# Expert choice behind the score transposes, rank products behind the value products, v ahead of q, and POOL's sum between its scatters

## What is computed

```
x  = x + fp8_ffn(lora_linear(x, cond_8))               # layer 0, gives x1
z  = x1 @ w_bot(cond_8) + bias                         # layer 1, one mixed weight per sequence
hn = layernorm(z);  q, k, v = hn @ wq, hn @ wk, hn @ wv
attn = softmax(q k / sqrt(8)) over 32 keys, 16 heads;  x' = z + attn v @ wo + bo
hn2 = layernorm(x');  idx = argmax(hn2 @ gate_w + gate_b)   # 8 experts, one per token
y  = x' + w2[idx] @ relu(w1[idx] @ hn2 + b1[idx]) + b2[idx];  out = x1 + y
```

## Time and profile before

| | |
|---|---|
| median of 3 runs | 324.71 us (321.15 to 331.06) |
| the profiled execution | 325.63 us, of it 323.8 us from the first to the last instruction |
| busy share of the span | PE 80%, DVE 67%, POOL 62%, ACT 60% |
| passes 5, 6 (L754 to the next L754) | 22.13 us, 21.47 us |
| granted TensorE clock, mean | 0.913 |

### The profile page before, as it was taken

The page is one execution under the profiler, slowest core; times in us unless marked ns, Lnnn a source line. Parts: engine busy times, 40 slices in busy tenths (PEclk is TensorE's granted clock), DMA queues, the critical chain, the costliest instruction groups (busy, mean ns, idle before and its releaser), DMA issues.

```text
span 323.8 us, 10450 instructions
## 1 busy us (share of the span) xinstructions
PE 259.3 (80%) x3558; PEld 201.6 (62%) x3565; DVE 215.6 (67%) x596; ACT 195.4 (60%) x422; POOL 199.4 (62%) x270
## 2 busy tenths in 40 slices
PE   4797889979979879799685876885849299999970
PEld 1454555755845656567465556774839289999970
DVE  4731499897988988988969777764743215565630
ACT  1556788795986986968946627325424036666640
POOL 1323265587786887887687655656674316878770
PEclk9977999999999999999988598579987859999996
DMA  5359100102002002010010051030241332333200
GB/s 191 121 170 436 47 3 2 37 0 79 25 10 90 0 33 81 0 65 5 2 65 5 2 157 43 2 95 29 80 142 50 101 88 55 99 93 104 89 22 0
DMA packets 12042, 22.01 MB, mean 68 GB/s; under 512 B 2508, under 2 KB 8656, under 8 KB 11744
## 3 DMA queue, kind: packets, MB, share of 16 engines
q1 hardware_dynamic: 8640, 14.63, 14.2%
q0 software_dynamic: 2784, 6.32, 5.7%
q10 hardware_dynamic: 576, 0.53, 0.5%
HBM read 13.97 MB, written 7.95 MB: 68 GB/s over the span
## 4 chain that ended last, share of the span: by engine, by line
PE 49%; DVE 23%; issue 11%; ACT 6%; DMA 4%; POOL 2%; SPq 1%; DVEq 1%; ACTq 0%; POOLq 0%
PE d L401 7%; PE d L413 6%; PE so L729 6%; PE so L401 5%; DVE mx L1171 5%; DVE pt L1189 4%; PE so L413 4%; DMA pack_sb<-pack 2%; PE d L805 2%; PE d L754 2%; PE d L788 2%; DVE pr L1175 2%; PE d L783 2%; PE so L716 2%; PE d L700 2%
## 5 line engine op out<-in xcount | busy, mean ns | idle before, releaser
L633 POOL DMA_INDIRECT out<-ob,rin x39 | 39.8, 1019 | 22.7 <-DVE w1s L551 12.6
L1456 POOL DMA_INDIRECT routed<-rows,slot x32 | 33.1, 1035 | 14.2 <-issue 9.1
L1378 POOL TENSOR_TENSOR t<-pr 128x512 f32<-128x512 f32 x16 | 20.5, 1282 | 15.4 <-ACT pr L958 15.3
L700 PE MATMUL d<-ybd,pack_sb 128*128 128x256 f32 x112 | 29.8, 396 | 0.0
L551 DVE COPY w1s<-pack_sb 128x644 f32 x39 | 22.3, 577 | 9.7 <-issue 4.0
L401 PE MATMUL d<-xt,w1s 128*128 128x128 f32 x168 | 26.8, 308 | 1.7 <-ACT xt L436 0.6
L413 PE MATMUL d<-pack_sb,mid 128*128 x168 | 27.3, 314 | 1.0 <-ACT mid L443 0.8
L436 ACT ACTIVATE xt<-d,pack_sb 128x128 f32<-128x128 f32 x21 | 9.6, 459 | 28.2 <-PE d L385 28.2
L401 PE MATMUL so<-xt,w1s 128*128 128x128 f32 x144 | 21.5, 295 | 6.3 <-issue 5.3
L413 PEld LDWEIGHTS d<-pack_sb,mid 128*128 128x128 f32 x168 | 24.6, 225 | 2.0 <-issue 1.8
L401 PEld LDWEIGHTS d<-xt,w1s 128*128 128x128 f32 x168 | 24.3, 220 | 2.5 <-issue 2.2
(11 more groups left out here) (184 smaller groups left out, 648.9 us busy)
## 6 DMA issues: line engine op xcount, KB each, us to landing
rin<-routed SPq DMA_DIRECT2D x39, 128.5 KB
pack_sb<-pack SPq DMA_DIRECT2D x1, 2576.0 KB, 15.2
xb<-x_t SPq DMA_DIRECT2D x8, 256.0 KB, 3.2
pack_sb<-pack SPq DMA_DIRECT2D x1, 2048.0 KB, 8.5
routed<-pad SPq DMA_DIRECT2D x5, 128.5 KB
out<-ob,rin POOLq DMA_INDIRECT x39
pack_sb<-pack SPq DMA_DIRECT2D x1, 584.0 KB, 6.2
routed<-pad ACTq DMA_DIRECT2D x4, 128.5 KB
```

Source lines behind the costliest of these rows:

```text
L633: pool.indirect_dma_start(out, bass.IndirectOffsetOnAxis(rin[s % 8][:, 2 * H:ROW].bitcast(U32), 0), ob[u][:, :], None, bounds_check=N_TOK ...
L700: mm = pe.matmul(mix_bank(a, k)[:, u * 256:(u + 1) * 256], col[f"mix_w{k // 2}"][:, (blk % 4) * P:(blk % 4 + 1) * P], ybd[:, :, :].rearran ...
L1378: pool.tensor_tensor(t16[:, f, :], e32[:, :, 0:16], e32[:, :, 16:32], ALU.add).then_inc(sem["sums"], 1)
L1456: pool.indirect_dma_start(routed, bass.IndirectOffsetOnAxis(slot[:, g:g + 1], 0), rows[:, g, :], None).then_inc(sem["scattered"], 16)
```

## The change

No operation is added or taken out. Four things move in the written order of the queues:

- DVE: `pick` moves from between the third and the fourth score block to behind the fourth transposition (in all passes that have attention work). `rank` moves from between the third and the fourth transposition to behind `eighth`, and `place` to behind the sum and reciprocal (L1320, L1325), with the first tables and copies of pass 8 behind it.
- TensorE: the rank products move from ahead of the k products to behind the value products. v's products go ahead of `coded`, and q's behind it: the last thing of a pass.
- ACT: the copies of v and q (`v_out`, `q_out`) swap places likewise. q's copy (L1077) was the first after L1073; now the order is reciprocals, v, q, `coded`.
- POOL: `x1` goes between the second and the third scatter, and with it the next pass's `spread`, so that the third and fourth scatter come behind both.

```diff
@@ TensorE @@
-                if m is not None:
-                    wait(pe, "pick", 6 * (m + 1))
-                    ... (rank products) ...
-                    mm.then_inc(sem["rank_mm"], 1)
                 if late(m) and m == NC - 2:
                     turn(2)
                     output(1)
                     hidden(2)
...
                     values(range(0, NG)).then_inc(sem["pv_mm"], 1)
+                if m is not None:
+                    wait(pe, "pick", 6 * (m + 1))
+                    ... (rank products) ...
+                    mm.then_inc(sem["rank_mm"], 1)
-                if n is not None:
-                    if m is not None:
-                        wait(pe, "slot", 5 * m + 2)
-                    pe.matmul(dn[0][:, :], col["wq"], hn_t[:, :], start=True, stop=True).then_inc(sem["qkv_mm"], 1)
-                if a is not None and not (isinstance(a, int) and a == 0):
-                    coded(a, n)
                 if n is not None:
                     wait(pe, "x1_tok", n + 1)
                     ... (v products) ...
                     mm.then_inc(sem["qkv_mm"], 1)
+                if a is not None and not (isinstance(a, int) and a == 0):
+                    coded(a, n)
+                if n is not None:
+                    if m is not None:
+                        wait(pe, "slot", 5 * m + 2)
+                    pe.matmul(dn[0][:, :], col["wq"], hn_t[:, :], start=True, stop=True).then_inc(sem["qkv_mm"], 1)
@@ ACT @@
-                if n is not None:
-                    wait(act, "qkv_mm", 3 * n + 2)
-                    act.activation(qt[:, :], dn[0][:, :], ACT.Identity, bias=col["bq"]).then_inc(sem["q_out"], 1)
                 ... (reciprocals, rcx) ...
+                if n is not None:
+                    wait(act, "qkv_mm", 3 * n + 2)
+                    wait(act, "pv_mm", n)
+                    act.activation(v[:, :, :], groups(dn[3][:, :]), ACT.Copy).then_inc(sem["v_out"], 1)
+                    wait(act, "qkv_mm", 3 * n + 3)
+                    act.activation(qt[:, :], dn[0][:, :], ACT.Identity, bias=col["bq"]).then_inc(sem["q_out"], 1)
                 if a is not None and not (isinstance(a, int) and a == 0):
                     coded(a)
@@ DVE @@
                     shifted(j, 2)
-                if m is not None:
+                if m is not None and j is None:
                     pick(m)
...
-                if m is not None:
-                    rank(m, p)
                 if isinstance(m, int) and m == SNAP:
                     first_pair()
                 if j is not None:
                     turned(j, 3)
+                if m is not None and j is not None:
+                    pick(m)
...
-                if m is not None:
-                    place(m)
-                if isinstance(m, int) and m == SNAP:
-                    first_b()
-                    for s in range(3):
-                        copy(s)
                 if a is not None:
                     eighth(a)
...
+                if m is not None:
+                    rank(m, p)
                 ... (sum, reciprocal) ...
+                if m is not None:
+                    place(m)
+                if isinstance(m, int) and m == SNAP:
+                    first_b()
+                    for s in range(3):
+                        copy(s)
@@ POOL @@
-                    for g in range(NG):
-                        pool.indirect_dma_start(...)
+                    scatter(0)
+                    scatter(1)
                 if a is not None:
                     ... (x1) ...
+                if a is not None and not (isinstance(a, int) and a == NC - 1):
+                    spread(a + 1)
+                if m is not None:
+                    scatter(2)
+                    scatter(3)
```

More of the change, by code:

```diff
@@ L877, in iteration @@
                     mm.then_inc(sem["hn_tr"], 1)
-                if m is not None:
-                    wait(pe, "pick", 6 * (m + 1))
-                    pe.matmul(gates(m)[:, 64:64 + NG * E], upper_b[:, :], oh_b[:, :, :].rearrange("p g e -> p (g e)"),
-                              start=True, stop=False, skip_group_check=True)
-                    for g in range(NG):
-                        mm = pe.matmul(gates(m)[:, 64 + (g + 1) * E:64 + (NG + 1) * E].rearrange("p (g e) -> p g e", e=E),
-                                       ones_b[:, :], oh_b[:, g, :].unsqueeze(1).to_broadcast([P, NG - g, E]),
-                                       start=False, stop=(g == NG - 1), skip_group_check=True)
-                    mm.then_inc(sem["rank_mm"], 1)
                 if late(m) and m == NC - 2:
@@ L914, in iteration @@
                     values(range(0, NG)).then_inc(sem["pv_mm"], 1)
+                if m is not None:
+                    wait(pe, "pick", 6 * (m + 1))
+                    pe.matmul(gates(m)[:, 64:64 + NG * E], upper_b[:, :], oh_b[:, :, :].rearrange("p g e -> p (g e)"),
+                              start=True, stop=False, skip_group_check=True)
+                    for g in range(NG):
+                        mm = pe.matmul(gates(m)[:, 64 + (g + 1) * E:64 + (NG + 1) * E].rearrange("p (g e) -> p g e", e=E),
+                                       ones_b[:, :], oh_b[:, g, :].unsqueeze(1).to_broadcast([P, NG - g, E]),
+                                       start=False, stop=(g == NG - 1), skip_group_check=True)
+                    mm.then_inc(sem["rank_mm"], 1)
                 if late(m) and m == NC - 2:
@@ L1084, in iteration @@
                     normed(3)
+                if n is not None:
[4 more added lines that the diff above has]
+                    act.activation(qt[:, :], dn[0][:, :], ACT.Identity, bias=col["bq"]).then_inc(sem["q_out"], 1)
                 if a is not None and not (isinstance(a, int) and a == 0):
                     coded(a)
-                if n is not None:
-                    wait(act, "qkv_mm", 3 * n + 3)
-                    wait(act, "pv_mm", n)
-                    act.activation(v[:, :, :], groups(dn[3][:, :]), ACT.Copy).then_inc(sem["v_out"], 1)
             def between(act):
@@ L1371, in rstd, with spread, scatter @@
                 pool.tensor_tensor(dst[:, 1, :], dst[:, 0, :], minus_half[:, :], ALU.pow).then_inc(sem[signal], 1)
+            def spread(a):
+                wait(pool, "wb_mm", 4 * a)
+                hold(pool, "held_pool")
+                pool.tensor_tensor(ybd[:, :, :],
+                                   col["y_rep"][:, bass.ds(a * CB, CB)].unsqueeze(1).to_broadcast([P, 16, CB]),
+                                   col["mask_o"].unsqueeze(2).to_broadcast([P, 16, CB]),
+                                   ALU.mult).then_inc(sem["ybd"], 1)
+            def scatter(g):
+                pool.indirect_dma_start(routed, bass.IndirectOffsetOnAxis(slot[:, g:g + 1], 0),
+                                        rows[:, g, :], None).then_inc(sem["scattered"], 16)
             def summed(j, half):
@@ L1388, in iteration @@
                     pool.wait_ge(sem["in1"], 16)
-                if a is not None:
-                    wait(pool, "wb_mm", 4 * a)
-                    hold(pool, "held_pool")
-                    pool.tensor_tensor(ybd[:, :, :],
-                                       col["y_rep"][:, bass.ds(a * CB, CB)].unsqueeze(1).to_broadcast([P, 16, CB]),
-                                       col["mask_o"].unsqueeze(2).to_broadcast([P, 16, CB]),
-                                       ALU.mult).then_inc(sem["ybd"], 1)
+                if isinstance(a, int) and a == 0:
+                    spread(0)
                 if isinstance(m, int) and m == SNAP:
@@ L1454, in iteration @@
                     hold(pool, "held_pool")
-                    for g in range(NG):
-                        pool.indirect_dma_start(routed, bass.IndirectOffsetOnAxis(slot[:, g:g + 1], 0),
-                                                rows[:, g, :], None).then_inc(sem["scattered"], 16)
+                    scatter(0)
+                    scatter(1)
                 if a is not None:
```

## The result

Changed kernel: median 339.84 us (6 runs, 335.77 to 344.86); kernel before, same chip: 328.13 us (6 runs). Ratio 1.049, 95% interval 1.033 to 1.065: slower. The profiled execution took 340.3 us against 325.63, 14.7 us more.

A forecast was written before the change was run, and what follows sets the result against it. No single engine bounds the loop; a ring of steps crossing engines does. Terms 2.5 + 3.4 + 1.8 + 3.5 + 1.5 = 12.7 us, against the median 324.71, gave 337.4, stated as 337.5 us; range 329.5 to 343.5.

The forecast's parts named there:

- the ring: Chain of steps crossing the engines, followed through pass 5, claimed to set the length of a loop pass.
- `rstd` "fits, with 0.3 to spare": POOL, loop passes: scatters end at V + 11.5, `rstd` due at V + 11.8; no cost, bound 0.5 us per pass.
- V sooner by 0.44: Loop passes: V, the start of the value products, comes 0.44 us sooner, limited by ACT's last exponential.
- q last, loop: Passes 3 to 6: q's late copy puts L754 at V + 5.8, `o_t` at V + 7.5; +3.4 us net.
- Passes 1 and 2: Front, without `pick`: v and `coded` stand ahead of q, nothing comes sooner; +2.5 us, bounds 1.0 and 3.0.
- Pass 7, "level": Pass 7's end: taken as unchanged, since with no further `a` no L754 follows its q.
- Pass 8, POOL: Pass 8: two scatters are put ahead of the tables of counts before `rstd`; +1.8 us, bounds 1.2 and 2.4.
- Pass 8, DVE: Pass 8: `rank` waits for rank products behind the values, postponed work delays the heads; +3.5 us, bounds 2.3 and 3.8.
- Pass 9: DVE: `place`, sum and reciprocal move behind the rank products, after the values' end; +1.5 us, bounds 0.5 and 1.8.
- ACT waits for the scatter to land: Passes 4 to 8: late scatter signal delays ACT's normalization row and exponentials 1 us each; +5, 342.5 us; chance 0.12.
- early values carry through: Passes 3 to 9: earlier value products take 1.4 us off each, q's copy hidden; 314.9 us; chance 0.03.
- only the front pays: Passes 8 and 9: TensorE hides POOL's table count and DVE's late work; only 5.9 us lost, 330.6; chance 0.14.

The follow-up runs named there:

- first pair: First profiles of the changed kernel and the kernel before, both unmodified: 340.3 us against 325.63.
- last chip: Both kernels run again unmodified: changed kernel 331.50 us, ratio 1.051; kernel before profiled again, 313.67 us (one run).
- v/q run: Kernel before with only the v/q order change on TensorE and ACT: 332.71 us, ratio 1.013.
- v/q runs: v/q order change alone on the kernel before, 332.71 us, ratio 1.013; and undone in the changed kernel, 335.81 us, ratio 1.049.
- late-passes run: Changed kernel with choice, rank products, `rank`, `place`, tables and copies of passes 8 to 10 put back: 332.36 us, ratio 1.035.

## Why the prediction was right or wrong

The direction and the ring were right, and the sum, 12.7 us, lies near the 14.7 of the two profiles. The step that failed is the one that put nothing down for the way behind `o_t`: `rstd` "fits, with 0.3 to spare". `o_t` to `nmr2` grew by 0.9 to 1.2 us in passes 4 to 6, which is 3.0 of the loop's 5.0 us, and by 0.9 in pass 7; the steps that had a price in the loop gave 2.0 us for 3.4. That the sum came near is in part luck, as errors in both directions met in it:

| us more than before | said | first pair | last chip |
|---|---|---|---|
| up to the first `o_t` | 2.5 | 2.3 | 2.4 |
| passes 3 to 6 | 3.4 | 5.0 | 5.3 |
| pass 7 | 0 | -0.2 | 1.3 |
| pass 8 | 5.3 | 6.2 | 5.2 |
| pass 9 | 1.5 | 3.2 | 0.8 |
| the rest | 0 | -1.8 | 1.8 |
| sum | 12.7 | 14.7 | 16.7 |

On the last chip the kernel before had one loop pass that was 1.6 us longer than its others; without it the loop's 5.3 would be 6.9.

- **V sooner by 0.44**: measured 0.5 to 0.6, with DVE idle ahead of the last transposition.
- **q last, loop**: L754 at V + 5.64 (said 5.8), reciprocals at V + 3.8 (3.7), `o_t` at V + 7.27 (7.5). Right, and shown alone by the v/q run. The reading "now 6.37" held 0.9 us of a late copy that other chips don't have; there the same step costs 1.8. One reading was wrong: in the kernel before `o_t` followed the end of DVE's heads (119.28 + 2.32 = 121.60, `o_t` at 121.64), and L764 had been done 0.1 us earlier. Only the change made TensorE's queue decide: DVE now waits 0.53 us for L764.
- **Passes 1 and 2**: from L754 to L754 +1.10 and +1.49, said 2.5 together; on the last chip +1.09 and +1.48, and the v/q runs show pass 2's 1.5 on two more.
- **`rstd` "fits, with 0.3 to spare"**: the step that failed. The first scatter starts 0.9 us after the slot numbers are ready (124.11 to 124.99), which the sum left out, so the last ends at V + 11.8 for 11.5, and `rstd` is directly behind it in passes 4 to 7. That costs the 0.2 to 0.6 us seen on the last chip, for which the prediction had a bound of 0.5 and no term. Above it came L805's lateness beside the fourth scatter, with no term at all: on the first chip the two made 0.9 to 1.2 us a pass. The bounds allowed 1.5 for a late row of the value products, so I had seen such lateness in the earlier trace rows, but did not ask what else would lie beside a scatter.
- **Pass 7, "level"**: level by luck. V came 1.3 us sooner behind `nmr2` (10.02 for 11.36), and `o_t` to `nmr2` 0.9 and V to `o_t` 0.3 us took it back; on the last chip the pass lost 1.3.
- **First scatter**: it went from 1.37 to 1.12 us, not to 0.96. By the Trainium skill's rule (SBUF — State Buffer, 🔬 SBUF: two separate sides) it would be 0.96; direction only. For two SBUF inputs that section has the lock only against a GpSimd operation that reads SBUF, a condition that the prediction did not name. No time hung on it.
- **Pass 8, POOL**: said 1.8 (1.2 to 2.4); `o_t` to `nmr2` grew by 2.3 (5.96 to 8.28), on the last chip by 1.8. The reason was only half of it: with POOL's order undone it is 8.29 as well, with POOL's order alone 7.16, and with the DVE part alone 7.58. The late `place`, which drives all four scatters and the tables behind them, is enough without POOL's order.
- **Pass 8, DVE**: said 3.5 (2.3 to 3.8), shown 3.6 to 3.9 by the late-passes run. The wait for the rank products, the unclosed gap of 1.25 and 5.1 us from values to heads (said 5.4) are there.
- **Pass 9**: said 1.5 (0.5 to 1.8), was 3.2. The priced step held: V to `o_t` grew by 1.5 (6.94 to 8.43). What had no term is 0.9 us behind `o_t`, where L783 ran at half clock (2.08 us for 1.16), and 0.8 from `nmr2` to V. The half clock is not the late `place` alone, for the late-passes run has the same 2.08. From `o_t` of pass 9 to that of pass 10 the mean granted clock was 0.62 (0.74 before) in the first pair and 0.85 (0.73 before) in the last, where both kernels differ by 0.75 us only (25.98 and 25.23): the term has the clock in it, in both directions. Why the end, level in the forecast, was 1.8 shorter in the first pair and 1.8 longer in the last is open; its mean clock was 0.90 in both kernels of the first pair, and on the last chip 0.91 in the changed and 0.92 in the kernel before.
- **Rival "ACT waits for the scatter to land"** (0.12): in part true. In the first profile one pass shows 0.79 us, on the last chip three show 0.6 to 1.2. The last scatter starts at V + 10.84, L1010 was due at V + 14.1: the spare was 3.3 us, near the 3.1 that I had, but where an engine waited for it the signal took 2.6 to 4.6. The Trainium skill (DMA: Bandwidth & Descriptors, 🔬 Anatomy of one DMA — SWDGE (gpsimd) path) gave an estimate of 2.3 for the scatter; the shortest that a run shows is 2.56. I had also listed such a wait as a sign against the forecast; it is an addition to it, not an alternative.
- **The other rivals** ("early values carry through", "only the front pays") fell: passes 3 to 6, 8 and 9 are all longer than before.

**Open.** Why a TensorE group's end is seen up to 1.7 us late beside a scatter, and only on some chips or executions. Moving the scatter away removes it; a plain sum was only tried where scatters did little either. What makes the scatter's signal take 2.6 us in one version and 4.6 in another is open too.

## What to carry to other kernels

Moving small work behind an engine's critical step moves everything that hangs on it: with `pick`, `rank` and `place` postponed the slot numbers came 3.5 us later behind V, and with them four DMA issues, a sum, the next pass's `rstd` and the DMA landing. Parts of a change like this are not to be summed: the DVE part alone cost as much as all three (1.051), and v and `coded` ahead of q fill a gap that it had opened. Before believing that a reading such as "V to `o_t` is 6.37" belongs to the code, profile the kernel on a second chip.
